# Gated cross-attention with a mixture of experts on one core: the experts' second biases folded into a spare part of a shared tile, and half of the weight loads put on ScalarE's queue

## The chip, the cores and the metric

The kernel runs on one core of one Trainium2 chip. The metric is the device time of one execution in microseconds (us); less is better. A time is stated for several executions of the same kernel, and the profile is of one further execution.

## What is computed

The input `x` is 4 x 256 rows of 256 numbers. Two blocks are added to it in turn, each scaled by the tanh of a gate. The first is cross-attention of 32 heads of 8 with rotary turns on queries and keys. The second is the part that the change touches: after a layer norm, two shared experts and 32 routed ones of hidden width 176, of which each row takes the 6 best.

```python
def expert(xf, w1, b1, w2, b2):
    return jnp.maximum(xf @ w1 + b1, 0.0) @ w2 + b2
shared = sum(expert(flat, *s) for s in shared_weights) / 2
probs = softmax(flat @ router_w + router_b)
p6, i6 = top_k(probs, 6);  p6 = p6 / sum(p6)
gates = zeros((1024, 32)).at[rows, i6].add(p6)
routed = sum(gates[:, e:e+1] * expert(flat, rw1[e], rb1[e], rw2[e], rb2[e]) for e in range(32))
x = x + tanh(g_ffn) * (shared + routed)
```

All data are float32, and the result is held to float32 accuracy. So large products are made of a high and a low part of each factor (three matmuls in a rounded float32 type for one product).

## The kernel before

The kernel is written by hand engine by engine; each engine has its own list of instructions, in a fixed order, and they meet by semaphores.

**Layout.** The 1024 rows (`TOK`) lie along the free dimension in the expert block, in two halves of 512 (`HALF`), one PSUM bank each. The hidden units of all experts are laid end to end and cut in tiles of 128: the two shared experts give 352 units, so two full tiles (`SFULL`) and one of 96 (`SREST`), the 32 routed experts give 5632, so 44 full tiles (`RT`). In all 47 tiles (`TILES`), numbered t; the routed ones are also numbered r = t - 3.

**One tile.** TensorE makes the hidden part (`hidden`, L1239): for each half, 6 matmuls of 512 columns (two parts of the model width times high-high, low-high, high-low) into `H_BANK`. For a routed tile VectorE then adds the first bias and multiplies by the gate (L925, writes `hu`; `hr` is the name of `hu[2]` and `hu[3]` in the shared tiles), ScalarE takes ReLU and rounds (L658, writes `hh`), and VectorE makes the low part (L931, writes `hl`). For a shared tile ScalarE does bias and ReLU (L605) and the rounding (L614) and VectorE or GpSimd the low part (L427, L908). Then TensorE makes the result part (`result`, L1256): 12 matmuls that add to the four banks `Y_BANK`, which hold the sum over all tiles until the end. GpSimd splits each tile's weights into high and low parts (L454 to L463), two tiles ahead by two buffers. TensorE's order is hidden part of tile t + 1, result part of tile t, and so on.

**The gates.** When the router's scores are there, VectorE makes `gates` (L901): per row 32 gates, and in two more columns the constant 1/2, written by GpSimd (L433). TensorE transposes them (`gates_transposed`, L1276), ScalarE copies the first half of the rows to `gTf` (L647) and VectorE the second (L914). SyncE stores `gTf` to DRAM (L310) and loads each tile's gate rows from there, each row repeated over the partitions of its expert, into a ring of four buffers `G` (L324, two loads a tile). From r = 4 on such a load waits until VectorE is done with the buffer (`hu_ok`).

**The second biases.** `b2_sb` holds 32 routed rows and 2 shared rows. After the result part of the third shared tile four float32 matmuls (L1294) add `b2_sb` times `gTf` to the four result banks. Since `gTf` holds the gates and twice 1/2, this is the whole of the second biases.

**The weight loads.** `load_weights(c)` loads half c of the routed experts' weights from SyncE's queue: two loads for `w1` (L302) and one for `w2` (L304). The first half is issued when attention is done (`norm_ok`), the second just before the gate load of tile r = 4, so after eight gate loads. GpSimd waits for a half (L444) before its first tile, r = 0 and r = 22.

**The order around the change**, on TensorE: hidden 2, gates transposes, result 1, hidden 3 (tile r = 0), result 2, bias matmuls, hidden 4, result 3 (tile r = 0), and from there the loop. On ScalarE: L605 and L614 of the third shared tile, then the loop of L658. At the end ScalarE (L662) and VectorE (L936) copy the result banks, TensorE transposes them back and VectorE adds the residual.

## Time and profile before

| | us |
|---|---|
| median of 3 runs | 435.04 |
| lowest, highest | 431.47, 436.26 |
| the profiled execution | 436.59 |
| its span, first to last instruction | 434.5 |
| TensorE busy in it | 416.2 |
| VectorE, ScalarE, GpSimd busy | 264.3, 192.0, 153.6 |

The profiled execution took 2.1 us more than its span; this is time ahead of the first and after the last instruction. All points of time in the rows are us from the start of the span. A busy share says how long an engine had an instruction in work, and not that its time set the end; which engine waited for which is read from the timelines. The mean granted clock of TensorE over the span was 0.986 of its full 2.4 GHz.

### The profile page before, as it was taken

The page shows a single profiled execution, that of the slowest core. Times are in us where ns is not written, and L with a number is a line of the kernel's source. Part 1 is how long each engine was busy: PE and PEld are TensorE (multiplying, and loading weights), DVE is VectorE, ACT ScalarE, POOL GpSimd, SP SyncE. Part 2 cuts the span into 40 slices and gives each one's busy share as a digit, 9 for nine tenths or more (in the row PEclk, how much of TensorE's full clock was granted, in tenths as well). Part 3 has the DMA queues.
Part 4 walks back from the last instruction along what each step waited for, and adds up shares of the span by engine and source line. Part 5 has one row for each costly group of instructions (what it writes and reads, how often), then busy time and mean ns, then how long its engine had stood idle before and what let it go on. Part 6 is the DMA issues. An engine that isn't in the chain of part 4 may idle for free.

```text
span 434.5 us, 8243 instructions
## 1 busy us (share of the span) xinstructions
PE 416.2 (96%) x2655; PEld 319.3 (73%) x2655; DVE 264.3 (61%) x525; ACT 192.0 (44%) x371; POOL 153.6 (35%) x295
## 2 busy tenths in 40 slices
PE   8799999999999899999999999999999999999995
PEld 5577666666665476768888888888888888888884
DVE  7987788788887376245555555555555555555554
ACT  4794999889888536222222222222222222222221
POOL 8455333211111034324444444444444444444430
PEclk9999999999999899969999999999999999999999
DMA  7300000000000089499933333333333333333102
GB/s 219 89 2 2 2 2 2 2 2 2 2 2 2 0 229 305 113 285 343 240 97 97 97 97 97 97 97 97 97 97 97 97 97 97 97 97 97 48 0 97
DMA packets 27960, 39.42 MB, mean 91 GB/s; under 512 B 3633, under 2 KB 22113, under 8 KB 27937
## 3 DMA queue, kind: packets, MB, share of 16 engines
q1 hardware_dynamic: 26897, 39.11, 32.3%
q8 instruction: 14, 0.23, 0.2%
q10 hardware_dynamic: 1040, 0.01, 0.1%
q14 instruction: 9, 0.07, 0.1%
HBM read 37.93 MB, written 1.18 MB: 90 GB/s over the span
## 4 chain that ended last, share of the span: by engine, by line
PE 63%; DVE 1%; ACT 0%; DVEq 0%; issue 0%; ACTq 0%
PE psum L1239 30%; PE psum L1256 29%; PE psum L1294 1%; PE psum L1215 1%; PE psum L956 0%; DVE attn L943 0%; PE psum L1209 0%; PE psum L1153 0%; PE psum L1276 0%; DVE xT L936 0%; DVEq L78 0%; PE psum L1141 0%; ACT Vx L574 0%; PE psum L1270 0%; PE psum L1113 0%
## 5 line engine op out<-in xcount | busy, mean ns | idle before, releaser
L658 ACT ACTIVATE hh<-hu 128x512 fp32r<-128x512 f32 x88 | 55.6, 633 | 189.6 <-DVE hu L925 189.5
L925 DVE SCALAR_TENSOR_TENSOR hu<-psum,b1cols,G 128x512 f32<-128x512 f32 x88 | 66.0, 751 | 112.8 <-PE psum L1239 106.1
L812 DVE TENSOR_REDUCE nmax<-psum 128x2 f32<-128x512 f32 x128 | 79.4, 684 | 10.6 <-PE psum L1055 9.9
L541 ACT ACTIVATE probs<-psum 128x512 f32<-128x512 f32 x128 | 69.4, 597 | 12.6 <-PE psum L1073 11.2
L1256 PE MATMUL psum<-hh,w2h 128*128 128x512 f32 (+1 forms) x188 | 73.2, 390 | 0.0
L1256 PE MATMUL psum<-hh,w2l 128*128 128x512 f32 (+1 forms) x188 | 73.2, 389 | 0.0
L1256 PE MATMUL psum<-hl,w2h 128*128 128x512 f32 (+1 forms) x188 | 73.1, 389 | 0.0
L931 DVE SCALAR_TENSOR_TENSOR hl<-hu,hh 128x512 fp32r<-128x512 f32 x88 | 60.9, 692 | 9.1 <-ACT hh L658 9.0
L460 POOL CAST w2h<-w 128x256 fp32r x44 | 17.9, 406 | 132.4 <-PE psum L1256 132.4
L1239 PE MATMUL psum<-xTh,w1h 128*128 128x512 f32 (+1 forms) x188 | 59.2, 396 | 0.0
L1239 PE MATMUL psum<-xTh,w1l 128*128 128x512 f32 (+1 forms) x188 | 58.8, 394 | 0.0
L1239 PE MATMUL psum<-xTl,w1h 128*128 128x512 f32 (+1 forms) x188 | 58.6, 393 | 0.0
L1055 PE MATMUL psum<-QK 32*128 32x256 f32 x256 | 38.9, 319 | 3.3 <-DVE nmax L812 2.8
L1239 PEld LDWEIGHTS psum<-xTh,w1h 128*128 128x128 f32 (+1 forms) x188 | 35.4, 190 | 8.8 <-issue 1.5
L1239 PEld LDWEIGHTS psum<-xTl,w1h 128*128 128x128 f32 (+1 forms) x188 | 35.7, 190 | 7.8 <-POOL xTl L439 0.2
L1239 PEld LDWEIGHTS psum<-xTh,w1l 128*128 128x128 f32 (+1 forms) x188 | 35.7, 190 | 7.7
L1256 PEld LDWEIGHTS psum<-hh,w2h 128*128 128x128 f32 (+1 forms) x188 | 35.4, 188 | 7.5
L1256 PEld LDWEIGHTS psum<-hl,w2h 128*128 128x128 f32 (+1 forms) x188 | 35.3, 188 | 7.3
L1256 PEld LDWEIGHTS psum<-hh,w2l 128*128 128x128 f32 (+1 forms) x188 | 35.3, 188 | 7.3
L1055 PEld LDWEIGHTS psum<-QK 32*128 32x128 f32 x256 | 25.8, 183 | 18.1 <-issue 10.5
L1073 PE MATMUL psum<-QT,QK 32*128 32x256 f32 x256 | 37.8, 329 | 0.9 <-ACT probs L541 0.8
L457 POOL TENSOR_TENSOR w1l<-w,w1h 128x256 fp32r<-128x256 f32 x44 | 32.5, 739 | 8.0 <-POOL w1h L454 8.0
(146 smaller groups left out, 492.7 us busy)
## 6 DMA issues: line engine op xcount, KB each, us to landing
G<-gates_by_expert SPq DMA_DIRECT2D x40, 256.0 KB, 4.1
w<-in_L_ffn_rw_dram SPq DMA_DIRECT2D x4, 1408.0 KB, 11.8
w<-in_L_ffn_rw_dram SPq DMA_DIRECT2D x2, 2816.0 KB, 18.1
G<-gates_by_expert SPq DMA_DIRECT2D x8, 448.0 KB, 3.8
G<-gates_by_expert SPq DMA_DIRECT2D x8, 384.0 KB, 3.5
G<-gates_by_expert SPq DMA_DIRECT2D x8, 320.0 KB, 3.5
G<-gates_by_expert SPq DMA_DIRECT2D x8, 192.0 KB, 3.9
x_sb<-in_x_dram SPq DMA_DIRECT2D x4, 256.0 KB, 4.4
```

Source lines behind the costliest of these rows:

```text
L457: pool.tensor_tensor(w1l[k][:, :, :], src1, w1h[k][:, :, :], ALU.subtract).then_inc(ws_ok, 1)
L460: pool.tensor_copy(w2h[k][:, :], src2).then_inc(ws_hi, 1)
L541: act.activation(probs[g % 2][:, :, n, :], st_bank(g, n)[:, :].rearrange("p (t q) -> p t q", t=TB), ACT.Exp, scale=SCALE).then_inc(exp_ok, 1)
L658: act.activation(hh[(SHT + j) % 2][:, cols], hu[2 * j + half][:, :], ACT.Relu).then_inc(rhh_ok, 1)
L812: dve.tensor_reduce(nmax[i % 2][:, :, n], S_BANK[(4 * i + n) % SB][:, :].rearrange("p (t k) -> p t k", t=TB), AX.X, ALU.max, negate=True). ...
L925: dve.scalar_tensor_tensor(out=hu[2 * (j % 2) + half][:, :], in0=H_BANK[2 * (j % 2) + half], scalar=b1cols[:, bass.ds(it * len(G) + j, 1)] ...
L931: dve.scalar_tensor_tensor(out=hl[k][:, cols], in0=hu[2 * (j % 2) + half][:, :], scalar=0.0, in1=hh[k][:, cols], op0=ALU.max, op1=ALU.subt ...
L1055: ins = pe.matmul(S_BANK[(4 * i + n) % SB][:, qt * N:(qt + 1) * N], QK[i % RING][h, 0, qt * P:(qt + 1) * P], QK[i % RING][h, 1, :], start= ...
L1073: ins = pe.matmul(st_bank(i, n)[:, kt * N:(kt + 1) * N], QK[i % RING][h, 1, kt * P:(kt + 1) * P], QT[i % 2][h, :], start=True, stop=True)
L1215: ins = pe.matmul(C_RTT[NE * b:NE * b + NE, 0:N], rtw_sb[:, k, :], xT32[:, k, N * b:N * b + N], start=(k == 0), stop=(k == KD - 1))
L1239: ins = pe.matmul(H_BANK[2 * pair + half][0:rows, :], w[k2][:, k, 0:rows], v[:, k, cols], start=(n == 0), stop=(n == len(parts) - 1))
L1256: ins = pe.matmul(Y_BANK[2 * k + half], w[k2][0:rows, wc], v[t % 2 if isinstance(t, int) else k2][0:rows, cols], start=(first and n == 0), ...
```

## The change

The second biases of the routed experts are loaded into the 32 rows that the third shared tile of `w2` leaves unused, and the transposed gates are copied into rows 96 to 127 of `hr`, where the hidden units of that tile would be. The third shared tile's copies, splits and result part now take all 128 rows, so its result part also adds gate times second bias. The gates are transposed from a tile of 128 columns whose first 96 are blank (zero, by GpSimd), so that they come out on partitions 96 to 127. ScalarE and VectorE copy them there when the low part of the tile that used `hr` before is made (`hl2_ok`), and the rounding of the third tile waits for them (`gTf_ok`). The four bias matmuls are gone. The mean of the two shared second biases is made by two matmuls of one column at the start, kept as two columns of `b1cols`, and added in the last copies of the result banks. The second half of the weights is issued by ScalarE after its last copy of the shared tiles, ahead of its loop, as four loads; the first half is four loads too, with `w2` cut in two. SyncE's gate loads go on without weight loads between them.

```diff
@@ setup @@
-    assert RT * P == NE * HID and HALF == BANK and C == P
+    assert RT * P == NE * HID and HALF == BANK and C == P and NS * HID % P + NE == P
...
-        b1cols = sb("b1cols", [P, TILES])
+        b1cols = sb("b1cols", [P, TILES + KD])
...
-        b2_sb = sb("b2_sb", [NE + NS, D])
+        sb2_sb = sb("sb2_sb", [NS, D])
+        mean = sb("mean", [NS, 1])
...
-        gates = sb("gates", [P, NT, NE + NS])
-        gTf = sb("gTf", [NE + NS, TOK])
+        gates = sb("gates", [P, NT, P])
@@ SyncE @@
-            sp.dma_start(b2_sb[0:NE, :], rb2).then_inc(b2_ld, 16)
-            sp.dma_start(b2_sb[NE:NE + NS, :], sb2).then_inc(b2_ld, 16)
+            sp.dma_start(sb2_sb[:, :], sb2).then_inc(b2_ld, 16)
...
+            sp.dma_start(w2s[SREST:P, SFULL, :], rb2).then_inc(ws_ld, 16)
...
-            load_weights(0)
+            for k in range(KD):
+                sp.dma_start(w1d[:, k, 0:NE // 2, :], w1v[:, k, 0:NE // 2, :]).then_inc(w_ld[0], 16)
+            for k in range(KD):
+                t0, t1 = k * RT // (2 * KD), (k + 1) * RT // (2 * KD)
+                sp.dma_start(w2[:, t0:t1, :], w2v[:, t0:t1, :]).then_inc(w_ld[0], 16)
             for half in range(2):
                 cols = slice(half * HALF, (half + 1) * HALF)
                 sp.wait_ge(gTf_ok[half], 1)
-                sp.dma_start(gd[:, cols], gTf[0:NE, cols]).then_inc(gd_st, 16)
+                sp.dma_start(gd[:, cols], hr[half][SREST:P, :]).then_inc(gd_st, 16)
             sp.wait_ge(gd_st, 32)
             for r in range(RT):
-                if r == len(G):
-                    load_weights(1)
@@ GpSimd @@
             pool.memset(b1rows[:, :], 0.0).then_inc(b1_clear, 1)
+            pool.memset(mean[:, :], 1.0 / NS).then_inc(half_ok, 1)
...
-                    pool.wait_ge(ws_ld, 16 * (KD + 2))
+                    pool.wait_ge(ws_ld, 16 * (KD + 3))
...
-                pool.tensor_copy(w2h[t][0:rows, :], w2s[0:rows, t, :]).then_inc(ws_hi, 1)
+                pool.tensor_copy(w2h[t][:, :], w2s[:, t, :]).then_inc(ws_hi, 1)
...
-            pool.memset(gates[:, :, NE:NE + NS], 1.0 / NS).then_inc(half_ok, 1)
+            pool.memset(gates[:, :, 0:SREST], 0.0).then_inc(blank_ok, 1)
...
-                pool.wait_ge(w_ld[c], 16 * (KD + 1))
+                pool.wait_ge(w_ld[c], 16 * 2 * KD)
@@ ScalarE @@
                 act.wait_ge(relu_ok, u + 1)
-                act.activation(hh[t % 2][0:rows, half * HALF:(half + 1) * HALF], hr[half][0:rows, :],
+                if t == SFULL:
+                    act.wait_ge(gTf_ok[half], 1)
+                act.activation(hh[t % 2][:, half * HALF:(half + 1) * HALF], hr[half][:, :],
                                ACT.Copy).then_inc(hh_ok, 1)
...
             act.wait_ge(gT_mm, 1)
-            act.activation(gTf[:, 0:HALF], GT_BANK[0][0:NE + NS, :], ACT.Copy).then_inc(gTf_ok[0], 1)
+            act.wait_ge(hl2_ok, 1)
+            act.activation(hr[0][SREST:P, :], GT_BANK[0][SREST:P, :], ACT.Copy).then_inc(gTf_ok[0], 1)
             for u in range(4, 6):
                 shared_relu(u)
                 shared_high_part(u)
...
+            for k in range(KD):
+                act.dma_start(w1d[:, k, NE // 2:NE, :], w1v[:, k, NE // 2:NE, :]).then_inc(w_ld[1], 16)
+            for k in range(KD):
+                t0, t1 = (KD + k) * RT // (2 * KD), (KD + k + 1) * RT // (2 * KD)
+                act.dma_start(w2[:, t0:t1, :], w2v[:, t0:t1, :]).then_inc(w_ld[1], 16)
             with act.Fori(0, RT // 2) as it:
...
-                act.activation(yT[:, 0, half * HALF:(half + 1) * HALF], Y_BANK[half][:, :], ACT.Copy).then_inc(yT_ok[half], 1)
+                act.activation(yT[:, 0, half * HALF:(half + 1) * HALF], Y_BANK[half][:, :], ACT.Identity,
+                               bias=b1cols[:, TILES:TILES + 1], scale=1.0).then_inc(yT_ok[half], 1)
@@ VectorE @@
-                    dve.tensor_copy(b1cols[:, :], A_B1[:, 0:TILES]).then_inc(b1_ok, 1)
+                    dve.tensor_copy(b1cols[:, :], A_B1[:, 0:TILES + KD]).then_inc(b1_ok, 1)
...
-            dve.wait_ge(half_ok, 1)
-            dve.tensor_tensor(gates[:, :, 0:NE], sel[:, :, :], per_expert(red[:, 1]), ALU.mult).then_inc(gates_ok, 1)
+            dve.tensor_tensor(gates[:, :, SREST:P], sel[:, :, :], per_expert(red[:, 1]), ALU.mult).then_inc(gates_ok, 1)
...
             dve.wait_ge(gT_mm, 2)
-            dve.tensor_copy(gTf[:, HALF:TOK], GT_BANK[1][0:NE + NS, :]).then_inc(gTf_ok[1], 1)
+            dve.wait_ge(hl2_ok, 2)
+            dve.tensor_copy(hr[1][SREST:P, :], GT_BANK[1][SREST:P, :]).then_inc(gTf_ok[1], 1)
...
-                dve.tensor_copy(yT[:, 1, half * HALF:(half + 1) * HALF], Y_BANK[2 + half][:, :]).then_inc(yT_ok[half], 1)
+                dve.tensor_scalar(yT[:, 1, half * HALF:(half + 1) * HALF], Y_BANK[2 + half][:, :],
+                                  b1cols[:, TILES + 1:TILES + 2], None, ALU.add).then_inc(yT_ok[half], 1)
@@ TensorE @@
+            pe.wait_ge(b2_ld, 16)
+            pe.wait_ge(half_ok, 1)
+            for k in range(KD):
+                pe.matmul(A_B1[:, TILES + k:TILES + k + 1], sb2_sb[:, k * P:(k + 1) * P], mean[:, :], start=True, stop=True)
             pe.transpose(A_B1[:, 0:TILES], b1rows[:, :], ident[0:TILES, 0:TILES]).then_inc(b1_mm, 1)
...
-                    ins = pe.transpose(GT_BANK[half][0:NE + NS, c * P:(c + 1) * P], gates[:, half * (NT // 2) + c, :], ident[:, :])
+                    ins = pe.transpose(GT_BANK[half][:, c * P:(c + 1) * P], gates[:, half * (NT // 2) + c, :], ident[:, :])
...
-            pe.wait_ge(half_ok, 1)
+            pe.wait_ge(blank_ok, 1)
...
-            result(SHT - 1, SHT - 1, SREST).then_inc(y_mm, 1)
-
-            pe.wait_ge(b2_ld, 32)
-            for half in range(2):
-                pe.wait_ge(gTf_ok[half], 1)
-                for k in range(KD):
-                    pe.matmul(Y_BANK[2 * k + half], b2_sb[:, k * P:(k + 1) * P],
-                              gTf[:, half * HALF:(half + 1) * HALF], start=False, stop=False, skip_group_check=True)
+            result(SHT - 1, SHT - 1, P).then_inc(y_mm, 1)
```

## Rows read from the trace of the kernel before

**Rows 1.** The page, busy us of each engine.
```profile
PE 416.2 (96%) x2655; PEld 319.3 (73%) x2655; DVE 264.3 (61%) x525; ACT 192.0 (44%) x371; POOL 153.6 (35%) x295
```

**Rows 2.** Timeline of TensorE: start, us, line, operands, count.
```profile
175.20 1.04 PE L1276 MATMUL psum<-ident,gates 128*34 128x128 f32 x8
...
178.82 0.62 PE L1239 MATMUL psum<-xTh,w1h 128*128 128x512 f32 x2
...
181.54 0.40 PE L1256 MATMUL psum<-hh,w2h 96*128 96x512 f32 x1
...
184.38 4.58 PE L1294 MATMUL psum<-gTf,b_sb 34*128 34x512 f32 x8
188.90 1.22 PE L1239 MATMUL psum<-xTh,w1h 128*128 128x512 f32 x2
...
194.05 0.40 PE L1256 MATMUL psum<-hh,w2h 128*128 128x512 f32 x1
```

**Rows 3.** Windows: length, busy us by engine, granted clock, DMA share, GB/s.
```profile
153.00:156.00 3.00, 2.45 (x18) 2.04 (x17) 2.81 (x12) 0.60 (x1) 0.32 (x2) 1.00 0.37 69
156.00:160.00 4.00, 4.00 (x29) 2.97 (x28) 2.66 (x10) 2.27 (x5) 0.71 (x1) 1.00 1.12 334
160.00:161.60 1.60, 1.60 (x12) 1.19 (x10) 1.49 (x6) 0.85 (x2) 0.19 (x1) 1.00 1.17 324
...
178.60:180.00 1.40, 1.40 (x8) 1.17 (x7) 0.69 (x1) 0.42 (x1) 0.76 (x1) 1.00 0.10 12
180.00:183.00 3.00, 3.00 (x15) 2.47 (x14) 0.00 (x0) 0.00 (x0) 1.82 (x3) 1.00 0.98 227
183.00:186.00 3.00, 3.00 (x11) 1.73 (x10) 1.80 (x3) 1.05 (x2) 1.12 (x3) 1.00 1.01 239
186.00:189.00 3.00, 3.00 (x6) 0.81 (x4) 1.35 (x2) 0.17 (x1) 1.75 (x3) 0.68 1.05 246
189.00:194.10 5.10, 5.10 (x13) 3.99 (x14) 0.75 (x1) 0.63 (x1) 0.00 (x0) 0.52 1.17 309
```

**Rows 4.** Timeline of VectorE, first routed tile.
```profile
183.99 1.41 DVE L925 SCALAR_TENSOR_TENSOR hu<-psum,b1cols,G 128x512 f32<-128x512 f32 x2 [4.25 <-DMA G<-gates_by_expert]
185.61 1.75 DVE L931 SCALAR_TENSOR_TENSOR hl<-hu,hh 128x512 fp32r<-128x512 f32 x2 [0.20 <-ACT hh L658]
```

**Rows 5.** Timeline of ScalarE, last shared copy and first routed one.
```profile
178.39 0.63 ACT L614 ACTIVATE hh<-hu 96x512 fp32r<-96x512 f32 x1
184.95 1.23 ACT L658 ACTIVATE hh<-hu 128x512 fp32r<-128x512 f32 x2 [5.93 <-DVE hu L925]
```

**Rows 6.** Timeline of SyncE's queue: DMA issues, start and us they took.
```profile
153.70 2.42 SPq L302 DMA_DIRECT2D w<-in_L_ffn_rw_dram  x2
156.16 5.44 SPq L304 DMA_DIRECT2D w<-in_L_ffn_rw_dram  x1
...
178.66 4.30 SPq L324 DMA_DIRECT2D G<-gates_by_expert  x8
183.00 6.70 SPq L302 DMA_DIRECT2D w<-in_L_ffn_rw_dram  x2
189.74 4.39 SPq L304 DMA_DIRECT2D w<-in_L_ffn_rw_dram  x1
```

**Rows 7.** GpSimd: a memset by line, and its timeline at 159 us.
```profile
L362 POOL MEMSET Vx<- 128x896 f32 x1 | 0.9, 902 | 0.0
...
159.06 0.71 POOL L353 TENSOR_TENSOR rough<-veps,halves 128x2 f32<-128x2 f32 x1 [5.22 <-DVE veps L722]
```

**Rows 8.** Timelines of TensorE and VectorE at the first biases' transpose.
```profile
27.98 0.26 PE L1122 MATMUL psum<-ident,b1rows 47*128 47x47 f32 x1
...
30.81 0.19 DVE L804 COPY b1cols<-psum 128x47 f32<-128x47 f32 x1
```

**Rows 9.** ScalarE's instructions of L662 and of L605.
```profile
L662 ACT ACTIVATE xT<-psum x2: 598/598/598, 426.8 to 428.2; 128x512 f32<-128x512 f32 x2
...
L605 ACT ACTIVATE hu<-psum,b1half x6: 669/677/689, 165.2 to 177.6; 128x512 f32<-128x512 f32 x4, 96x512 f32<-96x512 f32 x2
```

More of the change, by code:

```diff
@@ L210, in gated_cross_attention_moe @@
             sem(n) for n in ("half_ok", "ws_hi", "ws_ok", "h_mm", "relu_ok", "hh_ok", "hl_ok", "y_mm", "act_sync", "pool_sync"))
-        hl2_ok = sem("hl2_ok")
+        hl2_ok, blank_ok = sem("hl2_ok"), sem("blank_ok")
         hu_ok, rhh_ok, rhl_ok = (sem(n) for n in ("hu_ok", "rhh_ok", "rhl_ok"))
@@ L298, in _ @@
             w2v = rw2.rearrange("e h n -> (e h) n").rearrange("(t p) n -> p t n", p=P)
-            def load_weights(c):
-                e0, e1 = c * NE // 2, (c + 1) * NE // 2
-                for k in range(KD):
-                    sp.dma_start(w1d[:, k, e0:e1, :], w1v[:, k, e0:e1, :]).then_inc(w_ld[c], 16)
-                t0, t1 = c * RT // 2, (c + 1) * RT // 2
-                sp.dma_start(w2[:, t0:t1, :], w2v[:, t0:t1, :]).then_inc(w_ld[c], 16)
-            load_weights(0)
+            for k in range(KD):
[3 more added lines that the diff above has]
+                sp.dma_start(w2[:, t0:t1, :], w2v[:, t0:t1, :]).then_inc(w_ld[0], 16)
             for half in range(2):
@@ L405, in shared_low_second @@
             def shared_low_second(t):
-                rows = P if t < SFULL else SREST
                 pool.wait_ge(ws_hi, 2 * t + 2)
-                pool.tensor_tensor(w2l[t][0:rows, :], w2s[0:rows, t, :], w2h[t][0:rows, :], ALU.subtract).then_inc(ws_ok, 1)
+                pool.tensor_tensor(w2l[t][:, :], w2s[:, t, :], w2h[t][:, :], ALU.subtract).then_inc(ws_ok, 1)
             for g in range(GROUPS):
@@ L609, in shared_high_part @@
                 t, half = u // 2, u % 2
-                rows = P if t < SFULL else SREST
                 if t >= 2:
@@ L650, in _ @@
                 shared_high_part(u)
+            w1v = rw1.rearrange("e (k p) h -> p k e h", p=P)
+            w1d = w1[:, :, :].rearrange("p k (e h) -> p k e h", h=HID)
+            w2v = rw2.rearrange("e h n -> (e h) n").rearrange("(t p) n -> p t n", p=P)
+            for k in range(KD):
[3 more added lines that the diff above has]
+                act.dma_start(w2[:, t0:t1, :], w2v[:, t0:t1, :]).then_inc(w_ld[1], 16)
             with act.Fori(0, RT // 2) as it:
@@ L899, in _ @@
             then(dve.reciprocal(red[:, 1], red[:, 0]))
-            dve.wait_ge(half_ok, 1)
-            dve.tensor_tensor(gates[:, :, 0:NE], sel[:, :, :], per_expert(red[:, 1]), ALU.mult).then_inc(gates_ok, 1)
+            dve.tensor_tensor(gates[:, :, SREST:P], sel[:, :, :], per_expert(red[:, 1]), ALU.mult).then_inc(gates_ok, 1)
             def shared_low_part(u):
                 t, half = u // 2, u % 2
-                rows = P if t < SFULL else SREST
                 cols = slice(half * HALF, (half + 1) * HALF)
                 dve.wait_ge(hh_ok, u + 1)
-                dve.tensor_tensor(hl[t % 2][0:rows, cols], hr[half][0:rows, :], hh[t % 2][0:rows, cols],
+                dve.tensor_tensor(hl[t % 2][:, cols], hr[half][:, :], hh[t % 2][:, cols],
                                   ALU.subtract).then_inc(hl2_ok, 1)
@@ L1287, in _ @@
             hidden(SHT, SHT % 2, P, pair=0, r=0)
-            result(SHT - 1, SHT - 1, SREST).then_inc(y_mm, 1)
-            pe.wait_ge(b2_ld, 32)
-            for half in range(2):
-                pe.wait_ge(gTf_ok[half], 1)
-                for k in range(KD):
-                    pe.matmul(Y_BANK[2 * k + half], b2_sb[:, k * P:(k + 1) * P],
-                              gTf[:, half * HALF:(half + 1) * HALF], start=False, stop=False, skip_group_check=True)
+            result(SHT - 1, SHT - 1, P).then_inc(y_mm, 1)
             hidden(SHT + 1, (SHT + 1) % 2, P, pair=1, r=1)
```

## The prediction

> **What bounds the kernel now.** I read the page's busy shares first, then the timeline of each engine around the place that the change touches, then the windows. TensorE is busy for 416.2 of 434.5 us [rows 1]; its timeline shows what kind of busy this is. From the shared tiles on it runs 12 matmuls of a hidden part and 12 of a result part in turn with nothing between them: the hidden part that starts at 178.82 is followed by the next result part at 181.54, 2.72 us for 12 matmuls [rows 2]. So until the end every us that TensorE loses or saves around 184 us is lost or saved at the end, and ScalarE, VectorE and GpSimd matter only where TensorE must wait for them. Two things break the steady pace. The four bias matmuls of L1294, eight records, hold TensorE from 184.38 to 188.90, 4.52 us. The hidden part behind them takes from 188.90 to 194.05, 5.15 us for the same 12 matmuls [rows 2]: the granted clock was 0.68 in 186 to 189 and 0.52 in 189 to 194.1, so nearly all of it ran at 1.2 GHz and not at 2.4 [rows 3]. Before its fall TensorE did little but the bias matmuls, of 34 rows.
>
> **What is removed.** The bias matmuls go: -4.52 us. Their work is done by 32 more rows of the third shared tile; its result part already costs by columns (its 96-row records stand at 2.84 us between 181.54 and 184.38, against 2.72 for 128 rows), so more rows cost nothing on TensorE. If the low clock was a result of these matmuls, the hidden part behind them runs in 2.72: -2.43 us. Together -6.95 us, if the next thing in line is ready. The next thing is result part of routed tile 0, which began at 194.05 and could then begin at 184.38 + 2.72 = 187.1.
>
> **Is it ready?** It needs the first `hl` of that tile. The chain is gate rows landed, VectorE L925, ScalarE L658, VectorE L931: VectorE began at 183.99, when the gate rows had come (4.25 us of waiting for that DMA) [rows 4], ScalarE began at 184.95 [rows 5], and VectorE's two L931 ran 185.61 to 187.36 [rows 4]; the first is over at about 186.3. It is ready for 187.1, with 0.8 us to spare. But that holds only while ScalarE is free at 184.95 plus 0.8.
>
> **What is moved: four weight loads onto ScalarE's queue.** They are issued after ScalarE's last shared copy, which ends at 178.39 + 0.63 = 179.02 [rows 5]. On SP the issue of one half of the weights is not short: the first half took SP from 153.70 to 161.60, 7.90 us, with no other transfer in the queue; the second from 183.00 to 194.13, 11.13 us, behind eight gate loads [rows 6]. An issuing engine does nothing else meanwhile: SP's next gate load followed only then. What ended them? By its shapes the half is 2 x 1408 KB (w1) + 2816 KB (w2), 5.77 MB. By 161.60 had moved (3 x 69 + 4 x 334 + 1.6 x 324) / 1000 = 2.06 MB. By 194.1 had moved (1.4 x 12 + 3 x 227 + 3 x 239 + 3 x 246 + 5.1 x 309) / 1000 = 3.73 MB, of which 2.10 were the gate rows of four tiles, 128 rows of 4 KB each: 1.63 MB of weights [rows 3]. So in both cases the last issue returned when 1.6 to 2.1 MB of the half had gone and some 3.7 to 4.1 MB stood queued. I take this as the rule: the queue holds so much, and the issuer stands until the rest fits. That the last load is now cut in two changes nothing in the total, as both pieces are issued back to back.
>
> On ScalarE's queue the half starts to move about 1.3 us after the first issue (it was at 334 GB/s by 156, 2.3 us after 153.70, and had moved 0.2 MB by then), so at 180.3. Beside it go SP's eight gate pieces, issued from 178.66, and two more from about 185.4, when tile 0's `hu` are written: 2.62 MB at the 227 to 246 GB/s of the gate stretch [rows 3]. No row shows how two queues share. One end: the weights go first, 1.63 MB at 324 GB/s, ScalarE free at 185.3. Other end: the gate pieces go first, 2.62 MB at 240, then 2.06 MB at 324: 180 + 10.9 + 6.4 = 197.3. With equal bytes of some 280 GB/s, 1.63 to 2.06 MB take 11.6 to 14.7 us: 192 to 195. The middle of the ends is 191.3, that of the equal share 193.4; I take 192.5, 13.5 us after 179.02, somewhat above the 11.13 us that the second half took on SP with only the rest of the gate pieces ahead.
>
> The Trainium skill, page "DMA: Bandwidth & Descriptors", section "Queues, rings and completion order", says that each DMA engine takes turns between the queues, packet by packet; no row here shows it, and by it the value lies between the two ends. The same page, "Issuing engines are not separate DMA queues", says that issuing from several engines saves only sequencer time, "which is usually small relative to the DMA itself". SP's 7.90 and 11.13 us say otherwise for loads of this size [rows 6]; by the page's rule ScalarE would be free long before 185 and the sum would be -6.7 us.
>
> **Who stands behind the issues.** On ScalarE: L658 of tile 0, both halves. Behind them VectorE's L931 of tile 0 and, in its order, L925 of tile 1; behind these TensorE's result part 0, which is ahead of all the rest on TensorE. GpSimd waits for that result part before its next `w2h`, as now. With ScalarE free at 192.5, the first `hl` is there 0.63 + 0.03 + 0.69 = 1.35 us later [rows 4, 5], at 193.85, and the result part starts then: 0.2 us before 194.05. So nearly the whole 6.95 us goes into a wait of 193.85 - 187.1 = 6.7 us in which TensorE does nothing. I expect the clock to be low when it starts again. The low stretch that rows show cost 2.43 us over 12 matmuls [rows 2, 3]; I take 2.4 (bounds 0, if the clock holds, and 4.9, if 24 matmuls fall into it). From there the pace is as before. The gate loads of tile 4 on no longer stand behind the weights in SP's queue; TensorE did not wait for them before, so that gains nothing, but it also removes what would be late next in a kernel 7 us ahead.
>
> **Small terms.** The blanking memset of `gates` grows to 8 x 96 = 768 elements; GpSimd cleared 896 in 0.90 us, and it then sits idle for 5.22 us until the variances come [rows 7]: nothing. Without that cover it would be 0.8. The two one-column matmuls on `sb2` stand ahead of the transpose of L1122 at 27.98, whose reader L804 runs only at 30.81 [rows 8]: hidden, bounds 0 to 0.5. GpSimd's one more tiny memset and one load fewer ahead of the bias rows on SP: 0 to 0.1. The eight gates transposes, 1.04 us together [rows 2], load 128 columns for 34 but stream as many as now: 0 to 1.0, of which I take 0.1. At the end ScalarE's copy of 598 ns becomes one with a bias pointer, as L605 with 677 [rows 9]: 0.08, on the path once. Gate copy and `hh` of the third tile: ScalarE waits for VectorE's gate copy, which in the present order comes before it: 0. All together +0.2.
>
> **Sum.** -0.2 (result part 0) + 2.4 (clock) + 0.2 = +2.4 us. The profiled execution took 436.59 us (span 434.5 and 2.1 around it), which would become 439.0. The median of the runs is 435.04; I put the same difference on it: 437.4 us. About 1%, 4.35 us, is what a measurement of this kernel tells from no change, so this counts as no change.
>
> **Rivals.** (A) *ScalarE is not held.* The issues return early, because that queue has room or the weights go first, and ScalarE is free by 186. Then -6.95 + 0.2 = -6.7: 428.3 us. Free at 186.9, as SP would have been after its 7.90 us alone, with the clock held: result part 0 at 188.3, -5.8 + 0.2 = -5.6, 429.4. It is faster by over 1% up to 188, if the clock holds, and up to about 186 if not. For it: the first two issues of the first half took SP only 2.42 us [rows 6]. (The rule of the page speaks for it too.) Against it: the two long issues, and the gate pieces beside them. (B) *The gate loads win, or both queues are filled by one generator and hold each other up.* ScalarE is free at 197.3, result part 0 starts at 198.65, 4.6 us later than before, plus 2.4 and 0.2: +7.2, 442.2 us. It turns slower by over 1% from 194.6 on. For it: gate packets take the engines for long at 240 GB/s, and two more pieces arrive at 185.4. Against: the weights need only a third of their bytes moved. (C) *ScalarE is held until 190 to 192 but the clock holds*: -2.5 to -0.5, 433.5 us; it belongs with my forecast. Against it: the clock fell before though TensorE was not even idle.
>
> **How the numbers follow.** My forecast with C, all within 1%: 0.43. A: 0.27. B: 0.30. So faster 0.27, same 0.43, slower 0.30. The range goes from a part of A (free at 187, clock held) to B's own end: 429.5 to 443; the forecast's own range is 432 to 439.
>
> **What would show it.** Right: on ScalarE's queue four issues from 179 to about 192; L658 of tile 0 at about 192.5 instead of 184.95; TensorE idle for some 6 us before result part 0, released by VectorE; the next part at a clock near 0.5; no L1294. The first two issues should be short, the later two long. Wrong: L658 of tile 0 at 185 to 187, clock 1.0 throughout from 178 on, and TensorE without a gap (A); gate rows of tile 0 or 1 as the last releaser of L925 and ScalarE's issues beyond 195 (B). If TensorE is idle but L925 of tile 0 is what came late, the shared bandwidth and not ScalarE's issuing was the cause.

## The result, and the profile after

The changed kernel takes 445.83 us in the median (445.19 to 447.65, 4 runs), the kernel before, run beside it, 435.58 us (431.47 to 436.26). The ratio is 1.027, 95% interval 1.021 to 1.033: slower by some 10 us. The profiled execution took 445.19 us with a span of 443.2, 8.7 more than the 434.5 of before.

The timeline of TensorE in the changed kernel, where it answers to [rows 2] (L1249 is the hidden part, L1266 the result part):

```profile
177.57 0.62 PE L1249 MATMUL psum<-xTh,w1h 128*128 128x512 f32 x2
...
180.29 0.39 PE L1266 MATMUL psum<-hh,w2h 128*128 128x512 f32 x1
...
183.01 0.62 PE L1249 MATMUL psum<-xTh,w1h 128*128 128x512 f32 x2
...
200.81 0.76 PE L1266 MATMUL psum<-hh,w2h 128*128 128x512 f32 x1 [14.92 <-DVE hl L936]
...
205.45 0.62 PE L1249 MATMUL psum<-xTh,w1h 128*128 128x512 f32 x2
```

The bias matmuls are gone: the result part of the third shared tile starts at 180.29 and the hidden part behind it at 183.01, 2.72 us for 12 matmuls of 128 rows. This hidden part, which took 5.15 us before, takes 2.72 too. So both gains of the forecast are there. Then TensorE stands for 14.92 us until VectorE's `hl` of tile r = 0. The result part runs from 200.81 to 205.45, 4.64 us and not 2.72. The next hidden part starts at 205.45, and 196.78 in the trace before (194.05 + 2.73).

These terms add up to the 8.7 us between the spans: -4.5 (bias matmuls), -2.4 (hidden part at full clock), -0.1 (result part of the third tile at the pace of 128 rows), +15.1 (from 185.7 to 200.8), +1.9 (result part at low clock). The remaining -1.3 are no part of the change: already at the hidden part of 177.57 the changed kernel is 1.25 us ahead (178.82 before), and so at SyncE's first weight load (152.43 and 153.70); the window 140 to 150, in attention, had a granted clock of 0.83 before and 1.00 in the changed kernel.

The windows of the changed kernel, as in [rows 3] (length, busy us by engine, granted clock, DMA share, GB/s), show what the clock did:

```profile
180.00:185.70 5.70, 5.70 (x27) 4.54 (x25) 0.27 (x1) 0.00 (x0) 2.64 (x5) 1.00 1.07 261
185.70:200.80 15.10, 0.20 (x1) 0.02 (x1) 1.96 (x4) 1.15 (x2) 0.30 (x1) 0.68 1.09 280
200.80:205.40 4.60, 4.59 (x12) 3.67 (x13) 3.10 (x5) 1.24 (x2) 0.00 (x0) 0.58 1.09 348
205.40:208.20 2.80, 2.80 (x14) 2.27 (x14) 0.75 (x1) 0.09 (x1) 1.97 (x4) 1.00 1.11 321
```

The clock stays at 1.00 while TensorE works, falls while it stands idle, and is 0.58 in the first result part after it.

Why TensorE stood is in the timelines of ScalarE, as in [rows 5], and VectorE, as in [rows 4]. ACTq rows are ScalarE's own DMA issues: the start and the us that the issue took.

```profile
177.51 0.63 ACT L610 ACTIVATE hh<-hu 128x512 fp32r<-128x512 f32 x1
177.53 3.74 ACTq L652 DMA_DIRECT2D w<-in_L_ffn_rw_dram  x2
181.30 17.65 ACTq L655 DMA_DIRECT2D w<-in_L_ffn_rw_dram  x2
199.31 1.15 ACT L663 ACTIVATE hh<-hu 128x512 fp32r<-128x512 f32 x2 [21.17 <-issue]
```

```profile
185.43 1.41 DVE L930 SCALAR_TENSOR_TENSOR hu<-psum,b1cols,G 128x512 f32<-128x512 f32 x2 [6.49 <-DMA G<-gates_by_expert]
199.98 1.29 DVE L936 SCALAR_TENSOR_TENSOR hl<-hu,hh 128x512 fp32r<-128x512 f32 x2 [13.14 <-ACT hh L663]
```

The four issues occupy ScalarE from 177.53 to 198.95: 3.74 us for the first two, 17.65 for the last two. Its next copy, due at 186, starts at 199.31 and names "issue" as what it waited for, 21.17 us. VectorE began `hu` at 185.43, then waits 13.14 us for that copy, and TensorE waits for VectorE. The gate rows of tile 0 came 1.4 us later than before (185.43 for 183.99) though their loads were issued 1.3 us earlier (177.38 for 178.66): 2.7 us of delay, hidden behind ScalarE.

The last two issues (shortest, median, longest in ns) show that the third took 14.54 us and the fourth 3.08. Below them are the DMA queues from 183 to 191 (q1 is SyncE's queue, q10 ScalarE's: packets, MB, share of 16 engines):

```profile
L655 ACTq DMA_DIRECT2D w<-in_L_ffn_rw_dram x2: 3078/8810/14542, 181.3 to 195.9; - x2
```

```profile
q1 hardware_dynamic: 487, 1.60, 85.9%
q10 hardware_dynamic: 488, 0.34, 19.4%
```

In these 8 us the two queues got the same number of packets, 487 and 488. But a packet of gate rows has 4 KB and one of `w1` 704 bytes, so the gates got 1.60 MB and the weights 0.34.

Before that it was the other way round. The same view for 181 to 182 has only ScalarE's queue in the changed kernel, and the gates' 0.25 MB in the kernel before:

```profile
q10 hardware_dynamic: 426, 0.30, 115.7%
```

```profile
q1 hardware_dynamic: 70, 0.25, 105.0%
```

By 181 SyncE had issued more than five gate loads, and only the first had moved. The second, issued at 177.9, landed after 7.2 us, where it took 4.5 before. So the gate rows of tile 0 were late mostly because their queue stood still beside ScalarE's first loads. act_two and act_three show the same gap at 181 to 182; what held the queue is open.

### The profile page after: what moved, and what is told of

It is laid out like the page before. It is cut to its first block, busy times and chain, and to the rows that moved or that the text cites. A ratio compares the mean times of both kernels' runs of the same rounds, so it can differ in the third digit from the quotient of the medians.

```text
span 443.2 us, 8239 instructions
## 1 busy us (share of the span) xinstructions
PE 410.3 (93%) x2651; PEld 317.4 (72%) x2651; DVE 263.7 (60%) x525; ACT 192.3 (43%) x371; POOL 153.9 (35%) x296
## 4 chain that ended last, share of the span: by engine, by line
PE 53%; ACTq 5%; DVE 1%; ACT 0%; DVEq 0%; issue 0%
PE psum L1266 27%; PE psum L1249 26%; ACTq L655 4%; ACTq L652 1%; DVE attn L949 0%; DVE xT L941 0%; DVE hl L936 0%; DVEq L78 0%; ACT hh L663 0%; ACT hh L610 0%; ACTq L656 0%; ACTq L661 0%; ACTq L662 0%
## 5 line engine op out<-in xcount | busy, mean ns | idle before, releaser
L663 ACT ACTIVATE hh<-hu 128x512 fp32r<-128x512 f32 x88 | 55.6, 633 | 199.3 <-DVE hu L930 178.1
L1266 PE MATMUL psum<-hh,w2h 128*128 128x512 f32 x188 | 74.1, 394 | 14.9 <-DVE hl L936 14.9
L1266 PE MATMUL psum<-hh,w2l 128*128 128x512 f32 x188 | 73.9, 393 | 0.0
L1266 PE MATMUL psum<-hl,w2h 128*128 128x512 f32 x188 | 73.8, 393 | 0.0
L1249 PE MATMUL psum<-xTh,w1h 128*128 128x512 f32 (+1 forms) x188 | 58.1, 390 | 0.0
L1249 PE MATMUL psum<-xTh,w1l 128*128 128x512 f32 (+1 forms) x188 | 57.9, 389 | 0.0
L1249 PE MATMUL psum<-xTl,w1h 128*128 128x512 f32 (+1 forms) x188 | 57.9, 389 | 0.0
L1266 PEld LDWEIGHTS psum<-hh,w2h 128*128 128x128 f32 x188 | 35.8, 190 | 22.7 <-issue 15.3
L1266 PEld LDWEIGHTS psum<-hl,w2h 128*128 128x128 f32 x188 | 35.7, 190 | 7.6
L1266 PEld LDWEIGHTS psum<-hh,w2l 128*128 128x128 f32 x188 | 35.7, 190 | 7.4
L1249 PEld LDWEIGHTS psum<-xTh,w1l 128*128 128x128 f32 (+1 forms) x188 | 35.2, 187 | 7.5
L1249 PEld LDWEIGHTS psum<-xTl,w1h 128*128 128x128 f32 (+1 forms) x188 | 35.1, 187 | 7.6 <-POOL xTl L434 0.2
L1249 PEld LDWEIGHTS psum<-xTh,w1h 128*128 128x128 f32 (+1 forms) x188 | 35.0, 187 | 7.3
L458 POOL TENSOR_TENSOR w2l<-w,w2h 128x256 fp32r<-128x256 f32 x44 | 32.6, 741 | 8.0 <-POOL w2h L455 8.0
```

The source lines that it names most:

```text
L458: pool.tensor_tensor(w2l[k][:, :], src2, w2h[k][:, :], ALU.subtract).then_inc(ws_ok, 1)
L663: act.activation(hh[(SHT + j) % 2][:, cols], hu[2 * j + half][:, :], ACT.Relu).then_inc(rhh_ok, 1)
L1249: ins = pe.matmul(H_BANK[2 * pair + half][0:rows, :], w[k2][:, k, 0:rows], v[:, k, cols], start=(n == 0), stop=(n == len(parts) - 1))
L1266: ins = pe.matmul(Y_BANK[2 * k + half], w[k2][0:rows, wc], v[t % 2 if isinstance(t, int) else k2][0:rows, cols], start=(first and n == 0), ...
```

## The experiments

Ratios are to the kernel before, run on the same chip.

### Each half of the change by itself

**fold_sp**: the fold as in the change, the four loads of the second half on SyncE's queue, where they were before.

```diff
             for r in range(RT):
+                if r == len(G):
+                    for k in range(KD):
+                        sp.dma_start(w1d[:, k, NE // 2:NE, :], w1v[:, k, NE // 2:NE, :]).then_inc(w_ld[1], 16)
+                    for k in range(KD):
+                        t0, t1 = (KD + k) * RT // (2 * KD), (KD + k + 1) * RT // (2 * KD)
+                        sp.dma_start(w2[:, t0:t1, :], w2v[:, t0:t1, :]).then_inc(w_ld[1], 16)
...
-            for k in range(KD):
-                act.dma_start(w1d[:, k, NE // 2:NE, :], w1v[:, k, NE // 2:NE, :]).then_inc(w_ld[1], 16)
...
```

> The changed kernel with the second half's four weight loads back on SyncE's queue, ahead of the gate load of tile 4. Theory H (ScalarE is held by its own issues): ScalarE is free, its first routed copy comes at about 185 us and the first routed result part near 186.5, so 7.0 us are gained there against the kernel before (4.5 for the bias matmuls, 2.4 for the clock); but the gate rows of tile 4 still land near 207, behind the weights, and TensorE now comes 7 us earlier and waits some 3 us: about 432 us. Rival F (the fold itself, its waits between ScalarE and VectorE, costs the time): it stays near 445.

**queue_only**: the kernel before, bias matmuls and all, with the four loads on ScalarE's queue; `w2` of the first half is two loads too.

```diff
...
-                if r == len(G):
-                    load_weights(1)
...
             for u in range(4, 6):
                 shared_relu(u)
                 shared_high_part(u)
...
+            for k in range(KD):
+                act.dma_start(w1d[:, k, NE // 2:NE, :], w1v[:, k, NE // 2:NE, :]).then_inc(w_ld[1], 16)
+            for k in range(KD):
+                t0, t1 = (KD + k) * RT // (2 * KD), (KD + k + 1) * RT // (2 * KD)
+                act.dma_start(w2[:, t0:t1, :], w2v[:, t0:t1, :]).then_inc(w_ld[1], 16)
```

> The kernel before with only the queue of the loads changed: bias matmuls as they were, the second half's four loads issued by ScalarE after its last shared copy. Theory H: ScalarE is held from 179 to about 200, the first routed result part starts near 202 and not at 194, 8 us later, and some 2 us more for a low clock when TensorE starts again: about 445 us. Rival F: about 436, since the fold is not in it.

Measured: fold_sp 436.16 us, ratio 1.001 (0.998 to 1.005), 10 runs; queue_only 444.92, ratio 1.021 (1.015 to 1.028), 4 runs. So the queue of the loads alone costs about what the change costs (1.027), and the fold is not to blame. ScalarE's and TensorE's timelines of queue_only:

```profile
177.20 2.52 ACTq L654 DMA_DIRECT2D w<-in_L_ffn_rw_dram  x2
179.75 19.36 ACTq L657 DMA_DIRECT2D w<-in_L_ffn_rw_dram  x2
199.47 1.15 ACT L665 ACTIVATE hh<-hu 128x512 fp32r<-128x512 f32 x2 [21.65 <-issue]
```

```profile
183.20 3.70 PE L1301 MATMUL psum<-gTf,b_sb 34*128 34x512 f32 x8
186.82 0.74 PE L1246 MATMUL psum<-xTh,w1h 128*128 128x512 f32 x2
...
200.97 0.77 PE L1263 MATMUL psum<-hh,w2h 128*128 128x512 f32 x1 [11.09 <-DVE hl L938]
```

ScalarE is held from 177.20 to 199.1, and TensorE waits 11.09 us, less than the changed kernel's 14.92 because the bias matmuls fill a part: whatever TensorE does before, it starts at 201. (In this trace the hidden part behind the bias matmuls is over in 3.1 us, at a granted clock of 1.00. To this I come back at nofold_spread.)

fold_sp was expected at 432 and reached only 436. The timelines of TensorE, of VectorE and of SyncE's queue show why (the traced execution, 438.8 us, was the slowest of the ten, so its wait may be longer than usual):

```profile
215.38 0.79 PE L1264 MATMUL psum<-hh,w2h 128*128 128x512 f32 x1 [6.40 <-DVE hl L934]
```

```profile
183.66 1.41 DVE L928 SCALAR_TENSOR_TENSOR hu<-psum,b1cols,G 128x512 f32<-128x512 f32 x2 [3.40 <-DMA G<-gates_by_expert]
...
213.02 1.41 DVE L928 SCALAR_TENSOR_TENSOR hu<-psum,b1cols,G 128x512 f32<-128x512 f32 x2 [12.64 <-DMA G<-gates_by_expert]
```

```profile
190.06 7.89 SPq L315 DMA_DIRECT2D w<-in_L_ffn_rw_dram  x2
```

Tile 0 is on time (gate rows at 183.66, no wait of TensorE), but the gate rows of tile 4 come only at 213.02, after four weight loads whose last issue ended at 197.95. TensorE waits 6.40 us for tile 4, not 3. In the kernel before VectorE had these rows at 209.8; TensorE, 7 us later in its work, did not wait for them.

**fold_sp3** is fold_sp with `w2` of either half as one load, as before the change, which is the true undoing of the queue part. Against fold_sp (the first half is changed alike):

```diff
...
-                    for k in range(KD):
-                        t0, t1 = (KD + k) * RT // (2 * KD), (KD + k + 1) * RT // (2 * KD)
-                        sp.dma_start(w2[:, t0:t1, :], w2v[:, t0:t1, :]).then_inc(w_ld[1], 16)
+                    sp.dma_start(w2[:, RT // 2:RT, :], w2v[:, RT // 2:RT, :]).then_inc(w_ld[1], 16)
...
```

> The changed kernel's fold with the loads exactly as in the kernel before: w2 of a half as one load, the second half on SyncE ahead of the gate load of tile 4. Theory T (an issue returns about when the load two ahead has landed): SyncE is free near 194 and not at 198, the gate rows of tile 4 land near 209 and not 213, TensorE waits 2 to 3 us for them instead of 6.4: about 433 us. Rival R (fixed room): as with four loads, 436 us.

Measured: 435.3 us, ratio 1.001 (0.998 to 1.004), 10 runs.

```profile
181.58 7.08 SPq L310 DMA_DIRECT2D w<-in_L_ffn_rw_dram  x2
188.69 4.80 SPq L311 DMA_DIRECT2D w<-in_L_ffn_rw_dram  x1
193.54 132.61 SPq L321 DMA_DIRECT2D G<-gates_by_expert  x52
```

```profile
212.30 0.80 PE L1260 MATMUL psum<-hh,w2h 128*128 128x512 f32 x1 [4.80 <-DVE hl L930]
```

SyncE is free at 193.5 and not 198, as theory T had it, and TensorE waits 4.80 us where it waited 6.40. But the time did not become 433: the wait is longer than the 2 to 3 us expected, and after it the clock is low again (0.50 in 212.3 to 217, where 4.7 us of work stand for 2.35 at full clock). 4.8 and some 2.4 us are the fold's 7. That is a reason for moving the loads; what fails is to put all four on ScalarE's queue at once.

### What holds ScalarE

**act_two**: the changed kernel with only the two `w1` loads on ScalarE; `w2` goes on SyncE's queue ahead of tiles 8 and 10.

```diff
...
+                if r in (8, 10):
+                    n = KD + (r - 8) // 2
+                    t0, t1 = n * RT // (2 * KD), (n + 1) * RT // (2 * KD)
+                    sp.dma_start(w2[:, t0:t1, :], w2v[:, t0:t1, :]).then_inc(w_ld[1], 16)
...
-            for k in range(KD):
-                t0, t1 = (KD + k) * RT // (2 * KD), (KD + k + 1) * RT // (2 * KD)
-                act.dma_start(w2[:, t0:t1, :], w2v[:, t0:t1, :]).then_inc(w_ld[1], 16)
```

> The changed kernel, but ScalarE issues only the two w1 loads; the two w2 loads go on SyncE's queue ahead of the gate loads of tiles 8 and 10. Theory H (the third and fourth issue hold ScalarE, the first two take 3.7 us): ScalarE is free at about 181.5, its first routed copy waits only for the gate rows of tile 0 near 186, and TensorE loses 1 us or less: about 430 us. Rival B (the shared bandwidth, not the issuing, is what is late): the same turn-taking slows the gate rows, TensorE still waits 5 us or more and the time is over 435.

Measured: 432.28 us, ratio 0.994 (0.991 to 0.997), 10 runs.

```profile
177.37 3.91 ACTq L656 DMA_DIRECT2D w<-in_L_ffn_rw_dram  x2
186.48 1.22 ACT L664 ACTIVATE hh<-hu 128x512 fp32r<-128x512 f32 x2 [8.50 <-DVE hu L931]
```

```profile
187.98 0.77 PE L1267 MATMUL psum<-hh,w2h 128*128 128x512 f32 x1 [2.24 <-DVE hl L937]
```

The two issues end at 181.28 and ScalarE's copy waits for `hu` only, at 186.48. The weights on the other queue still slow the gate rows (VectorE had them at 185.5), and this is the whole price of the weight traffic beside them: TensorE waits 2.24 us, and not 14.92. So it was the third and fourth issue (14.54 and 3.08 us in the changed kernel), not the traffic. The time, 432.3, lies between the two expectations, as the low clock behind the short wait (0.60 in 188 to 192) was left out of both.

**act_three** and **act_eight**: the same data in three and in eight loads on ScalarE's queue (act_three has `w2` of either half as one load).

```diff
...
-            for k in range(KD):
-                t0, t1 = (KD + k) * RT // (2 * KD), (KD + k + 1) * RT // (2 * KD)
-                act.dma_start(w2[:, t0:t1, :], w2v[:, t0:t1, :]).then_inc(w_ld[1], 16)
+            act.dma_start(w2[:, RT // 2:RT, :], w2v[:, RT // 2:RT, :]).then_inc(w_ld[1], 16)
...
```

```diff
...
             for k in range(KD):
-                act.dma_start(w1d[:, k, NE // 2:NE, :], w1v[:, k, NE // 2:NE, :]).then_inc(w_ld[1], 16)
-            for k in range(KD):
-                t0, t1 = (KD + k) * RT // (2 * KD), (KD + k + 1) * RT // (2 * KD)
+                for c in range(2):
+                    e0, e1 = NE // 2 + c * NE // 4, NE // 2 + (c + 1) * NE // 4
+                    act.dma_start(w1d[:, k, e0:e1, :], w1v[:, k, e0:e1, :]).then_inc(w_ld[1], 16)
+            for c in range(4):
+                t0, t1 = RT // 2 + c * RT // 8, RT // 2 + (c + 1) * RT // 8
                 act.dma_start(w2[:, t0:t1, :], w2v[:, t0:t1, :]).then_inc(w_ld[1], 16)
```

> The changed kernel with w2 of each half as one load again, so three loads on ScalarE. Theory T (an issue returns about when the load two ahead of it has landed): the last of three returns when the first has landed, near 196, not 199: 3 us faster than the changed kernel, about 443 us. Rival R (the queue has room for a fixed amount, and the last issue returns when so much has moved, whatever the cutting): ScalarE is free at 199 as before, 446 us.

> The changed kernel with ScalarE's four loads cut into eight. Theory T: the eighth issue returns when the sixth load has landed, after 4.3 MB and not 2.9, so ScalarE is held until about 203.5 and the time is 4 to 5 us longer than the changed kernel's, about 450 us. Rival R (fixed room in bytes or packets): ScalarE is free at 199 as with four, 446 us.

Measured: act_three 443.7 us, ratio 1.019 (1.012 to 1.025), 4 runs; act_eight 448.16, ratio 1.031 (1.027 to 1.035), 2 runs. The interval of the changed kernel, 1.021 to 1.033, overlaps with either, but those of three and of eight loads do not overlap. The issues of the two, act_three first:

```profile
177.46 3.77 ACTq L650 DMA_DIRECT2D w<-in_L_ffn_rw_dram  x2
181.26 15.05 ACTq L651 DMA_DIRECT2D w<-in_L_ffn_rw_dram  x1
196.68 1.15 ACT L659 ACTIVATE hh<-hu 128x512 fp32r<-128x512 f32 x2 [18.60 <-issue]
```

```profile
177.65 13.61 ACTq L654 DMA_DIRECT2D w<-in_L_ffn_rw_dram  x4
191.29 9.44 ACTq L657 DMA_DIRECT2D w<-in_L_ffn_rw_dram  x4
```

Three loads hold ScalarE until 196.31, four until 198.95, eight until 200.73. What ScalarE's queue had moved at that moment, of 5.77 MB, act_three first:

```profile
q10 hardware_dynamic: 2558, 1.79, 40.4%
```

```profile
q10 hardware_dynamic: 4408, 3.14, 54.3%
```

So 1.79 MB with three loads, 3.14 with eight; the same view of the changed kernel gives 2.71 MB with four, of queue_only 2.68, of act_late4 below 2.80, and of SyncE's first half in the changed kernel, with nothing beside it, 2.71 by 162.42. On SyncE's queue fold_sp had moved 2.9 MB of the second half when its fourth issue returned, and three loads had moved 1.6 and 2.05 MB in the kernel before. So the amount is much the same for one way of cutting, on either queue and with or without other traffic (1.6 to 2.1 MB with three, 2.7 to 2.9 with four), and a finer cut makes it larger.

Theory T, that an issue returns when the load two ahead has landed, fits the third issue: act_three's returned at 196.3 and its first load landed at 196.4 (177.46 + 18.9); in the changed kernel both are at 195.9, on SyncE's first half at 159.4 and 159.5, and only queue_only is 1.2 us off (195.9 and 194.7). The fourth issue came 1.6 us before the second landing in the changed kernel (198.95 and 200.5). With eight loads T misses: the eighth issue returned at 200.73, when the fourth load landed (181.58 + 19.4 = 201.0), and the sixth landed only at 205.1. Rival R, one fixed amount, is out by three and by eight. What the queue counts stays open.

### Is it the engine, or the queue filled in one go?

**act_late4** and **act_one_each** keep all four loads on ScalarE. Its loop is written out for the first four tiles; act_late4 issues all four loads after tile 3, act_one_each one after each of the tiles 0 to 3 (`loads[r:r + 1]`). The cut of act_late4 leaves out where `loads` and `routed_copies`, the old loop body, are made.

```diff
-            with act.Fori(0, RT // 2) as it:
...
+            for r in range(4):
+                routed_copies(r // 2, r % 2)
+                for dst, src in (loads if r == 3 else []):
+                    act.dma_start(dst, src).then_inc(w_ld[1], 16)
+            with act.Fori(2, RT // 2) as it:
...
```

> The same, but all four loads in a row after the copies of tile 3, when only one tile's gate rows are loaded per 5.4 us. Theory H with turn-taking between the queues (the gate loads of five tiles lengthened the hold from the 10 us that the same four loads take on SyncE alone to 21): ScalarE is held for 10 to 13 us, 3.6 of them hidden, TensorE waits 7 to 9 us, with a low clock behind it about 438 us. Rival S (ScalarE's issues are slow by themselves, with or without gate loads): held 21 us again, about 446 us.

> The changed kernel's fold with the second half's four loads still on ScalarE's queue, but one after the copies of each of the tiles 0 to 3, where ScalarE has some 3.6 us free per tile. Theory H (ScalarE is held by the amount queued in its queue, not by issuing as such): each issue takes about 0.4 us, TensorE does not wait, 428 to 429 us, as with the loads spread on SyncE. Rival E (any large issue on ScalarE beside gate loads is long): ScalarE is held for several us per tile and the time is over 433.

Measured: act_late4 437.69 us, ratio 1.008 (1.005 to 1.011), 6 runs; act_one_each 428.36, ratio 0.989 (0.986 to 0.992), 7 runs.

```profile
197.80 14.90 ACTq L665 DMA_DIRECT2D w<-in_L_ffn_rw_dram  x4
213.06 1.15 ACT L661 ACTIVATE hh<-hu 128x512 fp32r<-128x512 f32 x2 [14.65 <-issue]
```

```profile
214.47 0.80 PE L1271 MATMUL psum<-hh,w2h 128*128 128x512 f32 x1 [6.74 <-DVE hl L941]
```

```profile
184.08 0.37 ACTq L665 DMA_DIRECT2D w<-in_L_ffn_rw_dram  x1
...
187.40 3.16 ACTq L665 DMA_DIRECT2D w<-in_L_ffn_rw_dram  x1
...
192.48 7.77 ACTq L665 DMA_DIRECT2D w<-in_L_ffn_rw_dram  x1
...
200.57 5.27 ACTq L665 DMA_DIRECT2D w<-in_L_ffn_rw_dram  x1
```

The same four issues in a row take 14.90 us beside the gate rows of two tiles, 21.4 beside those of five, and 10.0 on SyncE with nothing beside them (152.43 to 162.42 in the changed kernel). So the hold is no fixed cost of ScalarE's issuing, as rival S had it: it grows with what else the DMA engines must move while its queue drains. (14.90 is above the 10 to 13 expected; ScalarE's queue with nothing beside it was not run.) Spread over four tiles the issues still take 16.6 us together (0.37, 3.16, 7.77 and 5.27), not the 4 x 0.4 expected: the issues were several us long, as rival E had it, but the time was H's 428. Each fits, just, into the time that ScalarE has until TensorE needs its copy: behind the longest, ScalarE's copy starts at 200.41 and TensorE's result part at 202.24, on time. From 165 us on TensorE does not wait once, in this trace; two of the seven runs took 430.7 and 431.1.

### The version that beats both

**fold_spread**: the fold, with the four loads on SyncE's queue one at a time, ahead of the gate loads of tiles 5, 7, 9 and 11. **nofold_spread**: the kernel before with the same spread loads, and `w2` of either half as two loads. The cut is fold_spread's; nofold_spread puts the same loads at the same tiles.

```diff
...
+                if r in (5, 7, 9, 11):
+                    n = (5, 7, 9, 11).index(r)
+                    if n < KD:
+                        sp.dma_start(w1d[:, n, NE // 2:NE, :], w1v[:, n, NE // 2:NE, :]).then_inc(w_ld[1], 16)
+                    else:
+                        t0, t1 = n * RT // (2 * KD), (n + 1) * RT // (2 * KD)
+                        sp.dma_start(w2[:, t0:t1, :], w2v[:, t0:t1, :]).then_inc(w_ld[1], 16)
...
```

> The changed kernel's fold, with the second half's four loads on SyncE's queue one at a time, ahead of the gate loads of tiles 5, 7, 9 and 11. Theory H: nothing holds ScalarE, the gate rows of tiles 0 to 4 have no weights before them, TensorE does not wait once from 165 us to the end and the clock stays high there: the 7.0 us of bias matmuls and low clock are kept, 428 us. Rival (part of the 7 us is lost elsewhere, by the later gate rows or by a clock that falls anyway): 430 to 434.

> The kernel before with the same spread loads, bias matmuls as they were. Theory H: the second half's loads cost the kernel before nothing, so it stays at 435, and the difference to the fold with spread loads is what the fold is worth, 7 us (4.5 for the matmuls, the rest for the clock). Rival: the spread itself is what gains, then this kernel is near 430.

Measured: fold_spread 428.2 us (428.1 to 428.65, 5 runs), ratio 0.985 (0.982 to 0.988); nofold_spread 433.34 (431.41 to 435.3, 12 runs), ratio 0.998 (0.995 to 1.000). The issues of fold_spread, and one of its windows:

```profile
185.14 0.44 SPq L313 DMA_DIRECT2D w<-in_L_ffn_rw_dram  x1
...
193.47 0.42 SPq L313 DMA_DIRECT2D w<-in_L_ffn_rw_dram  x1
...
204.34 0.43 SPq L316 DMA_DIRECT2D w<-in_L_ffn_rw_dram  x1
...
215.54 0.59 SPq L316 DMA_DIRECT2D w<-in_L_ffn_rw_dram  x1
```

```profile
180.00:187.00 7.00, 7.00 (x33) 5.79 (x32) 3.91 (x5) 1.23 (x2) 3.81 (x7) 1.00 1.04 246
```

Each issue takes 0.4 to 0.6 us; no other weight load is in the queue then (they land in 10 to 11 us). TensorE is busy without a gap and at clock 1.00 in this window, and in those before and behind (165 to 210). Neither half of this gains by itself: the fold with the loads in a row is at 1.001 (fold_sp3), the spread loads without the fold at 0.998, both together at 0.985. In nofold_spread the bias matmuls are there, and the low clock behind them too:

```profile
182.48 4.27 PE L1300 MATMUL psum<-gTf,b_sb 34*128 34x512 f32 x8
186.68 1.22 PE L1245 MATMUL psum<-xTh,w1h 128*128 128x512 f32 x2
...
191.97 0.56 PE L1262 MATMUL psum<-hh,w2h 128*128 128x512 f32 x1
```

The matmuls take 4.20 us and the hidden part behind them 5.29 and not 2.72: 6.8 us over a kernel with the fold, as in the kernel before. The medians of the two differ by 5.1 us. queue_only shows why that can be less: there the same bias matmuls took 3.62 us (183.20 to 186.82) and the clock did not fall, so they cost 3.6 us and their follower little. The low clock at this place came in two of the three traces that have the bias matmuls, and in none that lacks them. The mean granted clock of nofold_spread's runs goes with their times: 434.5 to 435.3 us at 0.990, 431.4 to 431.7 at 1.000. That fits a loss of clock that comes in some executions only, but where in these runs the clock fell is on no record, and scatter alone is no sign of it: fold_sp and fold_sp3, without the bias matmuls, scatter by 5.3 and 4.3 us. Why the clock fell in two traces and held in one was not tried.

## Why the prediction was wrong

The place, the engine and the direction of the cost were as written, the size was not: the forecast was 437.4 us, "no change", and the measured 445.8 lies above the range's end of 443.

**What held.** The removed work: 4.5 us of bias matmuls and 2.4 us of clock came back between the two traces, to the tenth. (Over many executions it is less, 5.1 us by the medians of the two spread kernels: a term of clock read from one execution holds for that execution.) That a result part of 96 rows costs no less than one of 128: 2.84 us before, 2.72 after. That ScalarE, and behind it VectorE's L931 and L925, and TensorE's result part 0, would stand behind the issues, the first two short (3.74 us) and the last two long (17.65, of which the third has 14.54). That the clock would be low afterwards: 1.9 us lost, where 2.4 was taken. That the gate rows of tile 4 "would be late next in a kernel 7 us ahead": fold_sp3 shows it, 4.80 us. The small terms: no row shows a wait at any of them, and the sum of the terms above leaves nothing for them.

**The step that failed** is ScalarE's release, "I take 192.5": it was 199.3, a hold of 21.4 us and not 13.5, as the issues began 1.5 us earlier than taken. So TensorE's wait was 14.9 us and not 6.7. Two terms stood behind the release.

First, "the last issue returned when 1.6 to 2.1 MB of the half had gone", with "that the last load is now cut in two changes nothing in the total". The 1.6 to 2.1 MB were right for three loads (act_three: 1.79), but the changed kernel has four, and with four the last issue returns at 2.7 to 2.9 MB, on either queue. The cut itself lengthened the hold: 0.9 MB at 320 GB/s is 2.9 us, and act_three ended its hold 2.6 us earlier and took 2 us less than the changed kernel in the median and in the trace. The rows of before could not show this, as both halves had the same cut; a bound of the kind "until all but the last load has gone" was missing.

Second, the sharing, which was taken as nearly equal in bytes. From 183 to 191 it is equal in packets, 487 and 488, and so 1.60 to 0.34 MB. The end of the range, "the gate pieces go first", was nearer the truth for this stretch, though some 0.7 MB of weights had moved before it. The sizes of the packets, 4 KB and 704 bytes, follow from the shapes and could have been compared beforehand.

The two do not add up one by one. With three loads, where the amount was as taken, the release is at 196.3 (act_three): the 3.8 us over 192.5 come from the sharing. With four loads the amount alone gives the release, however the queues share: equal bytes make 180.3 + 2.71 / 0.14 = 199.7 us, and the gates first make 180 + 10.9 + 2.71 / 0.324 = 199.3, as by then the gate rows are through either way. Measured 199.3. That it agrees so closely is in part luck: the gates' first load was issued 1.3 us earlier than these sums have it, and the rate of both queues together was lower, 262 GB/s from 178.6 to 198.95.

The Trainium skill, page "DMA: Bandwidth & Descriptors", section "Queues, rings and completion order", says that a DMA engine takes turns between queues packet by packet. The trace agrees from 183 to 191, with 487 and 488 of what the profile counts as packets, and not before, when the gates' queue had loads issued and moved nothing (181 to 182). Read with the packet sizes the rule would have pointed to the end of the range and away from equal bytes. The same page's sentence in "Issuing engines are not separate DMA queues", that sequencer time for issuing is usually small relative to the DMA itself, does not hold here: 21.4 us for four loads of 1.4 MB, of which the last landed 33.7 us after the first was issued.

**The rivals.** B came nearest ("the gate loads win", from 183 on), and its mechanism gave 442.2; with 199.3 in the place of 197.3 the same sum gives 444.2, 1.6 us short of the median. Its second clause, that both queues are filled by one generator and hold each other up, was not needed for ScalarE's hold, and no run tests it. SyncE's issuing was hardly longer, 4.90 us for eight gate issues (177.38 to 182.28) for 4.30 before, but the issued gate loads stood still at 181 to 182, and this is what such a hold of one queue by the other would look like. It is most of why the gate rows of tile 0 were late, which cost TensorE 2.24 us in act_two. A was wrong: ScalarE is not free at 186 or 188 in either kernel that has four loads in a row at this place, nor with three or eight. The argument for it, two short issues, says nothing about the third.

## What to carry to other kernels

A large load (1.4 MB here) cost the engine that issued it 0.4 to 0.6 us with no other in its queue, 2 to 3 us behind one such load, and 4 to 16 us behind two, until about the landing of the first: put large loads on a compute engine's queue one at a time, or leave them on SyncE and spread them between the small loads that others wait for. When two queues are busy, compare their packet sizes before the bytes: the one with the small packets got a sixth of the bytes from 183 to 191 here. And when a stretch ahead of a just hidden transfer gets shorter, look at that transfer first; the gain here became 1.5% of the time only after the weight loads had been taken out of the way of the gate rows.

## What the runs showed of the hardware that was not expected

Cutting the same 5.77 MB into more loads made the issuer stand longer, at the same place and beside the same traffic: until 196.3 us with three, 198.95 with four, 200.7 with eight, with 1.79, 2.71 and 3.14 MB moved. And the queue's limit is not a fixed number of bytes or of packets, since at those moments 4.0, 3.1 and 2.6 MB stood unmoved, and some 4400, 3100 and 2600 packets. Nor does the other queue go on as before: for some 2 us behind ScalarE's first issues the gate loads already issued on SyncE's queue moved nothing.
